# The add of the two halves of V's products, moved from VectorE to GpSimd

## The chip, the core and the metric

The kernel runs on one core of a Trainium2 chip. The metric is the device time of one execution in microseconds, as the median of several runs. The engines of the core that matter here are TensorE (PE in the profile; PEld are its weight loads), VectorE (DVE), ScalarE (ACT), GpSimd (POOL) and SyncE (SP), which only issues transfers. Each works through its own instructions in order, and they wait for each other by semaphores.

## What is computed

An attention block over 16 images of 32 x 32 pixels with 512 channels, all in f32:

```python
xn = silu(group_norm(x, gn_scale, gn_offset))        # 32 groups
q, k, v = split(einsum('bxyc,cd->bxyd', xn, w_qkv), 3)   # 8 heads of 64
sim = einsum('bhdi,bhdj->bhij', q * 64 ** -0.5, k)   # 1024 x 1024 per head
out = einsum('bhij,bhdj->bhid', softmax(sim), v)
return einsum('bxyd,dc->bxyc', out, w_out) + b_out + x
```

## The kernel before

TensorE multiplies f16 operands. To come near f32, each operand is split into a high f16 part and a low one (what the high part left over), and the products of high with high, high with low and low with high are summed in PSUM.

One image is 64 units. A unit is one of eight heads, one half of its 1024 queries and one quarter of its keys (256 keys): `v // 8` is the head, `v // 4 % 2` the half of the queries, `v % 4` the quarter of the keys. Four units are a half: after them the product of the probabilities with V is complete for 512 queries of one head. `step(b, s, ...)` holds 16 units of image `b`; the text counts units of an image from 0 to 63, unit 33 is step 2, `u` = 1. The loop runs over two images at a time and is written out once for every engine, so the order on each is fixed by the code; the tables `TURNS`, `BN_AT`, `Z_AT`, `TANH_AT`, `SILU_FROM` and the like say in which unit side work is done. While image `b` goes through the attention, the group norm, the SiLU and the projections of image `b + 1` are done between.

What each engine does in unit `v`:

- TensorE: the scores (lines 1133 and 1134, into `ST`); the product of the unnormalised scores for a later maximum (line 1045, into `TP`); half of a side job, six passes of a projection (line 1031, into `SD`); and the product of the probabilities of unit `v - 2` with V (line 1163, into `PV`). After units 1, 5, 9, ... it also spreads the shift of a later half over the partitions (line 1052, into `TP`), for which it waits for `ms`.
- ScalarE: the exponentials twice, in f32 (`P`, line 666) and in f16 (`Ph`, line 669); the high part of a side job (`QK` line 623, `V` line 628); `z` and tanh for the SiLU (lines 650, 657). In every unit with `v % 4 == 2` it first copies the finished half from `PV` to `pv_sum` (line 677).
- VectorE: the low part of a side job (lines 769, 774, 781); its half of the low probabilities, `Pl = P - Ph` of unit `v - 1` (line 865); in units with `v % 4 == 3` the function `sums`; the maximum over `TP` (line 828) and, after the fourth maximum of a group, `ms` (line 798). When TensorE has spread the shift, VectorE copies it into `QK2` (line 832).
- GpSimd: the other half of `Pl` of unit `v - 1` (line 553); in units with `v % 4 == 3` the function `normalise`; in units 26 to 47 the SiLU of the next image, three operations in two units (lines 530, 533, 537, 540, each 128x512, from `z` and `th` to the high and low part of `xn`); the bias on the residual (line 545); and once an image the Newton steps and coefficients of the group norm.

V lies in SBUF with its high part, a column of ones, and its low part beside each other: 64 + 1 + 64 columns. The high probabilities are multiplied with all of them, the low ones with the first 65. `PV` thus holds for each of four query blocks a sum for the high part (64 columns), the denominators (one column, `HD`) and a sum for the low part (64 columns from `LO` = 65). The last block has its low part added within PSUM already, so three blocks are left to be added. `pv_sum` (f32, two buffers, by `half % 2`) receives them, `den` the reciprocals of the denominators. `normalise` writes four blocks into `O32`, which TensorE transposes later (line 1105) for the output projection.

The semaphores around it: ScalarE's copy raises `pv_out`; VectorE waits for it in `sums` and raises `den_ready`; GpSimd waits for that in `normalise` and raises `o_normed`; ScalarE waits for `o_normed` before it overwrites the buffer of two halves ago, and TensorE before it transposes. GpSimd's `Pl` raises `lo_pool`, for which TensorE waits before line 1163 and ScalarE before it overwrites `P`.

Of the kernel before, what the change touches and what calls it, by code (L numbers as in the profile page):

```python
# [10 lines left out]
ALU = mybir.AluOpType  # L11
# [4 lines left out]
HEADS, HD = 8, 64  # L16
# [6 lines left out]
LO = HD + 1  # L23
# [23 lines left out]
def rows_of(hh):  # L47

    return slice(hh * HD, hh * HD + HD)
# [151 lines left out]
def wait(eng, sem, count):  # L201

    if not isinstance(count, int) or count > 0:
        eng.wait_ge(sem, count)


def conv_attention(nc, x, gamma, beta, w_qkv, w_out, b_out, out):
# [4 lines left out]
    with ctx:  # L212
        def sb(name, shape, dt):
            return ctx.enter_context(nc.sbuf_tensor(name, shape, dt))
# [4 lines left out]
        def sem(name):  # L219
            return ctx.enter_context(nc.semaphore(name))  # L220
# [48 lines left out]
        pv_sum = sb("pv_sum", [P, 2, 4, LO + HD], F32)  # L269
        den = sb("den", [P, 2, 4], F32)  # L270
# [69 lines left out]
        pv_done = sem("pv_done")  # L340
        pv_out = sem("pv_out")
        den_ready = sem("den_ready")
        o_normed = sem("o_normed")

        def wait_placed(eng, pairs):
# [122 lines left out]
        def _(pool):  # L468
# [86 lines left out]

            def normalise(b, half):

                pool.wait_ge(den_ready, 16 * b + half + 1)
                pair, hh, q = half // 4 % 4, half // 2 % 2, half % 2
                if hh == q == 0:  # L560

                    wait(pool, ot_filled, 4 * b + half // 4 - 1)
                nc.gpsimd.tensor_tensor(O32[:, pair % 2, 4 * q:4 * q + 4, rows_of(hh)],  # L563
                                        pv_sum[:, half % 2, :, 0:HD],
                                        den[:, half % 2, :].unsqueeze(2).to_broadcast([P, 4, HD]), ALU.mult
                                        ).then_inc(o_normed, 1)

            def step(b, s, par, first=False, last=False):
                for u in range(16):
                    v = 16 * s + u  # L570
                    if not (first and v == 0):
                        low_probs(b, v - 1)
                    if v % 4 == 3 and not (first and v == 3):
                        normalise(b, v // 4 - 1)
                    if (s, u) == NEWTON_AT and not last:
                        newton(b + 1)
                        coefficients(b + 1)
                    for i, op in [] if last else silu_ops(s, u):
                        silu(b + 1, 1 - par, i, op)
                    if (s, u) in BIAS_AT:  # L580
                        add_bias(b, BIAS_AT[s, u])
                    if (s, u) in LATE_BIAS_AT and not first:
                        add_bias(b - 1, LATE_BIAS_AT[s, u])
# [8 lines left out]
            with nc.Fori(0, B // 2 - 1, engines=[pool.engine], hint_back_edge=True) as two:  # L592
                b = two * 2
# [10 lines left out]
            for s in range(4):  # L604
                step(B - 1, s, 1, last=True)
            low_probs(B - 1, UNITS - 1)
            normalise(B - 1, 15)
            for t in range(4, 8):
                add_bias(B - 1, t)
# [129 lines left out]
        def _(dve):  # L739
# [128 lines left out]
            def sums(b, half):  # L868


                dve.wait_ge(pv_out, 16 * b + half + 1)
                nc.vector.reciprocal(den[:, half % 2, :], pv_sum[:, half % 2, :, HD])
                nc.vector.tensor_tensor(pv_sum[:, half % 2, 0:3, 0:HD], pv_sum[:, half % 2, 0:3, 0:HD],  # L873
                                        pv_sum[:, half % 2, 0:3, LO:LO + HD], ALU.add).then_inc(den_ready, 1)

            def step(b, s, par, cnt, first=False, last=False):
                turned = []
                for u in range(16):
                    v = 16 * s + u
                    if (s, u) == AGGREGATE_AT and not last:  # L880
                        dve.wait_ge(bn_done, b + 2)
                    for use in (shift_before(s, u, last) if not (first and v == 0) else []):
                        top_use(use, b + 1, cnt)
                    for use in job_before(s, u, first, last):
                        side(use, image_of(use, b, s), cnt)
                    for use, slot in turned:
                        low_output(use[1], image_of(use, b, s), slot)
                    if not (first and v == 0):
                        low_probs(b, v - 1)
                    if v % 4 == 3 and not (first and v == 3):  # L890
                        sums(b, v // 4 - 1)
                    for use in unit_max(s, u, last):
                        top_use(use, b + 1, cnt)
                    cnt.next_slot()
                    turned = [(use, cnt.next_slot()) for use in unit_turn(s, u, first, last)]
                    turned = [(use, slot) for use, slot in turned if use[0] == "ot"]
                    if not last:
                        if (s, u) in BN_AT:
                            for i in BN_AT[s, u]:
                                channel_stats(b + 1, 1 - par, i)  # L900
                        if (s, u) == AGGREGATE_AT:
                            aggregate(b + 1)
                for use in unit_job(s, 15, first, last):
                    side(use, image_of(use, b, s), cnt)
# [97 lines left out]
            with nc.Fori(0, B // 2 - 1, engines=[dve.engine], hint_back_edge=True) as two:  # L1002
                b, now = two * 2, cnt.later(two * 2)
# [11 lines left out]
            for s in range(4):  # L1015
                step(B - 1, s, 1, now, last=True)
            low_probs(B - 1, UNITS - 1)
            sums(B - 1, 15)
            low_output(3, B - 1, now.next_slot())
            for t in range(TB):  # L1020
# [244 lines left out]
```

## Time and profile before

| | us |
|---|---|
| median of 3 runs | 3793.7 |
| lowest and highest | 3792.2 and 3794.3 |
| the profiled execution, its own time | 3788.9 |
| its span in the trace | 3787.1 |
| TensorE busy (matmuls) | 3622.2 (96%) |
| VectorE busy | 3211.4 (85%) |
| ScalarE busy | 2816.3 (74%) |
| GpSimd busy | 2309.0 (61%) |

The granted clock of TensorE is 0.99 of full speed in the mean over the span, and nine tenths or more in every slice of the page but the first. The shares are means over an image whose parts differ: they say which engine is near its limit, not which one is waited for at a given place. For that the waits and the timelines are read. The idle time of an engine is put down to what released it last. A duration on VectorE or GpSimd includes the time in which the instruction had begun but could not yet reach its operands, so the same operation on the same shape may be short in one place and long in another.

### The profile page before, as it was taken

What the parts mean: (1) busy time and instruction counts of PE and PEld (TensorE: products, weight loads), DVE (VectorE), ACT (ScalarE), POOL (GpSimd) and SP (SyncE); (2) the same over time, 40 slices, a digit from 0 to 9 for tenths busy, and PEclk for the clock granted to TensorE, in tenths of its full rate; (3) what the DMA queues carried; (4) which work ended last, traced back from release to release, by engine and by line L of the source; (5) the groups of instructions that cost most, each with busy time, mean ns of one, the idle gap of its engine ahead of it and who ended that gap; (6) DMA issues with size and microseconds to landing.
All of it is one profiled execution on the core that took longest, in us unless ns stands there. A gap on an engine that the chain in (4) does not pass through costs nothing.

```text
span 3787.1 us, 92715 instructions
## 1 busy us (share of the span) xinstructions
PE 3622.2 (96%) x32844; PEld 2103.6 (56%) x32844; DVE 3211.4 (85%) x4027; ACT 2816.3 (74%) x3074; POOL 2309.0 (61%) x2211
## 2 busy tenths in 40 slices
PE   5899999999999999999999999999999999999997
PEld 2555555555555555555555555555555555555553
DVE  6888888888888888888888898888988888888885
ACT  3777777778777787777777777787777877777774
POOL 1383855838467494765838567494764847558444
PEclk7999999999999999999999999999999999999999
DMA  2112113132131222213132121221212222131221
GB/s 92 53 39 77 55 46 85 35 91 57 46 85 40 68 57 71 60 40 87 38 82 62 48 73 40 83 57 53 78 40 68 57 74 57 46 85 35 68 57 34
DMA packets 120776, 228.89 MB, mean 60 GB/s; under 512 B 12672, under 2 KB 29056, under 8 KB 120320
## 3 DMA queue, kind: packets, MB, share of 16 engines
q1 hardware_dynamic: 120320, 222.87, 21.9%
q8 instruction: 279, 4.57, 0.5%
q14 instruction: 177, 1.45, 0.1%
HBM read 71.57 MB, written 33.55 MB: 28 GB/s over the span
## 4 chain that ended last, share of the span: by engine, by line
PE 73%; DVE 14%; issue 7%; ACT 4%; DMA 1%; POOL 0%; DVEq 0%; SPq 0%; ACTq 0%; POOLq 0%
PE SD L1031 26%; PE PV L1163 14%; PE ST L1133 9%; PE ST L1134 9%; PE TP L1045 9%; DVE mx L828 5%; DVE Pl L865 3%; DVE ms L798 2%; PE TP L1052 2%; PE ST L1098 1%; ACT Ph L669 1%; PE ST L1105 1%; DVE st L842 1%; ACT th L657 1%; DVE res L781 1%
## 5 line engine op out<-in xcount | busy, mean ns | idle before, releaser
L553 POOL TENSOR_TENSOR Pl<-P,Ph 128x512 f16<-128x512 f32 x1024 | 1265.1, 1236 | 1171.6 <-ACT Ph L669 1170.5
L666 ACT ACTIVATE P<-ST,cns 128x1024 f32<-128x1024 f32 x1024 | 1141.1, 1114 | 780.0 <-PE ST L1134 767.6
L828 DVE TENSOR_REDUCE mx<-TP 128x1 f32<-128x1024 f32 x1024 | 1244.9, 1216 | 171.9 <-PE TP L1045 168.6
L669 ACT ACTIVATE Ph<-ST,cns 128x1024 f16<-128x1024 f32 x1024 | 1133.7, 1107 | 0.0
L865 DVE TENSOR_TENSOR Pl<-P,Ph 128x512 f16<-128x512 f32 x1024 | 1028.5, 1004 | 9.3 <-ACT Ph L669 6.1
L1163 PE MATMUL PV<-V,Ph 128*128 128x129 f16 (+2 forms) x10240 | 862.5, 210 | 4.4 <-POOL Pl L553 1.6
L1163 PEld LDWEIGHTS PV<-V,Ph 128*128 128x128 f16 x10240 | 771.8, 97 | 125.9 <-ACT pv_sum L677 8.9
L1163 PE MATMUL PV<-V,Pl 128*128 128x65 f16 x8192 | 835.0, 192 | 0.0
L1163 PEld LDWEIGHTS PV<-V,Pl 128*128 128x128 f16 x8192 | 723.1, 98 | 110.3 <-issue 1.1
L1134 PE MATMUL ST<-QK 128*128 128x512 f16 x2048 | 777.5, 380 | 2.6 <-issue 2.6
L1133 PE MATMUL ST<-QK 128*128 128x512 f16 x2048 | 777.6, 380 | 0.3 <-ACT Ph L669 0.2
L1031 PE MATMUL SD<-X,wq 128*128 128x512 f16 x3048 | 745.2, 381 | 21.5 <-POOL X L521 15.6
L1045 PE MATMUL TP<-QK 128*128 128x512 f16 x2048 | 610.4, 380 | 14.7 <-DVE mx L828 11.7
L1031 PEld LDWEIGHTS SD<-X,wq 128*128 128x128 f16 x3048 | 291.0, 98 | 403.0 <-DVE QK L769 47.7
L1031 PE MATMUL SD<-wo,OT 128*128 128x512 f16 x1536 | 374.7, 381 | 10.9 <-DVE res L781 8.4
L1031 PE MATMUL SD<-wq,X 128*128 128x512 f16 x1488 | 361.4, 379 | 1.3 <-DVE wq L929 1.3
L1133 PEld LDWEIGHTS ST<-QK 128*128 128x128 f16 x2048 | 202.6, 99 | 184.0 <-issue 1.9
L1134 PEld LDWEIGHTS ST<-QK 128*128 128x128 f16 x2048 | 200.2, 98 | 181.6 <-issue 1.3
L769 DVE SCALAR_TENSOR_TENSOR QK<-SD,sc,QK 128x512 f16<-128x512 f32 x254 | 190.2, 749 | 118.6 <-ACT QK L623 102.4
L832 DVE CAST QK<-TP 64x512 f16<-64x512 f32 x256 | 176.1, 688 | 133.8 <-PE TP L1052 132.1
L563 POOL TENSOR_TENSOR O<-pv_sum,den 128x256 f32<-128x256 f32 x256 | 157.6, 616 | 199.1 <-DVE pv_sum L873 199.1
L1031 PEld LDWEIGHTS SD<-wo,OT 128*128 128x128 f16 x1536 | 149.0, 98 | 199.7 <-DVE res L781 19.1
(110 smaller groups left out, 3222.3 us busy)
## 6 DMA issues: line engine op xcount, KB each, us to landing
QK<-QK SPq DMA_DIRECT2D x384, 256.0 KB, 4.9
res<-in_x SPq DMA_DIRECT2D x128, 256.0 KB, 2.8
out<-res SPq DMA_DIRECT2D x128, 256.0 KB, 2.0
x_in<-in_x SPq DMA_DIRECT2D x61, 512.0 KB, 3.9
V<-V SPq DMA_DIRECT2D x16, 1040.0 KB, 6.4
V<-in_L_conv_w_qkv SPq DMA_DIRECT2D x4, 768.0 KB, 11.0
P<-in_L_conv_w_out SPq DMA_DIRECT2D x1, 1024.0 KB, 14.7
z<-in_x SPq DMA_DIRECT2D x1, 512.0 KB, 6.1
```

Source lines behind the costliest of these rows:

```text
L553: nc.gpsimd.tensor_tensor(Pl[:, v % 4, HALF:], P32[:, v % 2, HALF:], Ph[:, v % 4, HALF:], ALU.subtract).then_inc(lo_pool, 1)
L666: nc.scalar.activation(P32[:, v % 2, :], ST[:, slot, :], ACT.Exp, scale=cns[:, 0:1])
L669: nc.scalar.activation(Ph[:, v % 4, :], ST[:, slot, :], ACT.Exp, scale=cns[:, 0:1]).then_inc(exp_done, 1)
L769: nc.vector.scalar_tensor_tensor(out=QK[:, lo, cols], in0=bank, scalar=sc[:, col:col + 1], in1=QK[:, hi, cols], op0=ALU.mult, op1=ALU.subt ...
L828: nc.vector.reduce_max(mx[:, hh, qb:qb + 1], TP[:], AX.X).then_inc(top_drained, 1)
L832: nc.vector.tensor_copy(QK2[r, head_slot(pair, hh), 0, bass.ts(half, HALF)], TP[r, 0:HALF]).then_inc(top_drained, 1)
L865: nc.vector.tensor_tensor(Pl[:, v % 4, 0:HALF], P32[:, v % 2, 0:HALF], Ph[:, v % 4, 0:HALF], ALU.subtract).then_inc(lo_dve, 1)
L1031: ins = nc.tensor.matmul(bank, stationary(i, c), moving(j, c), start=(c == 0 and i + j == 0), stop=(c == CC - 1 and i == 1))
L1045: ins = nc.tensor.matmul(TP[:, bass.ts(kh, HALF)], QK1[:, slot, 0, bass.ts(qb, P)], QK1[:, slot, 1, bass.ts(kh, HALF)], start=True, stop=True)
L1133: nc.tensor.matmul(dst, QK1[:, at, 1, kb], QK1[:, at, 0, bass.ts(q, HALF)], start=True, stop=False)
L1134: ins = nc.tensor.matmul(dst, QK2[:, at, 1, kb], QK2[:, at, 0, bass.ts(q, HALF)], start=False, stop=True)
L1163: ins = nc.tensor.matmul(PV[:, cols], stationary, moving, start=kb == qb == n == 0, stop=kb == TB - 1, skip_group_check=True)
```

## The change

In `sums` VectorE keeps the reciprocals and raises `den_ready` behind them. The add of the three low parts to the high parts, in place in `pv_sum`, goes to the head of `normalise` on GpSimd, behind a wait of its own for `pv_out`. A new semaphore, `pv_added`, lets GpSimd's normalisation wait for GpSimd's own add; behind it stands the wait for `den_ready` as before. Shapes and types are the same. The order of everything else on the five engines stays.

```diff
--- before.py
+++ after.py
@@ -340,6 +340,7 @@
         pv_done = sem("pv_done")
         pv_out = sem("pv_out")
         den_ready = sem("den_ready")
+        pv_added = sem("pv_added")
         o_normed = sem("o_normed")
 
         def wait_placed(eng, pairs):
@@ -555,6 +556,10 @@
 
             def normalise(b, half):
 
+                pool.wait_ge(pv_out, 16 * b + half + 1)
+                nc.gpsimd.tensor_tensor(pv_sum[:, half % 2, 0:3, 0:HD], pv_sum[:, half % 2, 0:3, 0:HD],
+                                        pv_sum[:, half % 2, 0:3, LO:LO + HD], ALU.add).then_inc(pv_added, 1)
+                pool.wait_ge(pv_added, 16 * b + half + 1)
                 pool.wait_ge(den_ready, 16 * b + half + 1)
                 pair, hh, q = half // 4 % 4, half // 2 % 2, half % 2
                 if hh == q == 0:
@@ -869,9 +874,7 @@
 
 
                 dve.wait_ge(pv_out, 16 * b + half + 1)
-                nc.vector.reciprocal(den[:, half % 2, :], pv_sum[:, half % 2, :, HD])
-                nc.vector.tensor_tensor(pv_sum[:, half % 2, 0:3, 0:HD], pv_sum[:, half % 2, 0:3, 0:HD],
-                                        pv_sum[:, half % 2, 0:3, LO:LO + HD], ALU.add).then_inc(den_ready, 1)
+                nc.vector.reciprocal(den[:, half % 2, :], pv_sum[:, half % 2, :, HD]).then_inc(den_ready, 1)
 
             def step(b, s, par, cnt, first=False, last=False):
                 turned = []
```

On VectorE, in units 35 and 36 (`Pl` of unit 34, then `sums`, the maximum, the low part of a side job). Before:

```order
L865 TENSOR_TENSOR Pl<-P,Ph 128x512 [waits pv_done]
L871 ISA
L872 RECIPROCAL den<-pv_sum 128x4 [waits pv_out]
L873 TENSOR_TENSOR pv_sum<-pv_sum 128x3x64
L803 REGISTER_ALU
L828 TENSOR_REDUCE mx<-TP 128x1 [waits top_filled]
L759 REGISTER_ALU
L762 REGISTER_ALU [waits side_filled]
L769 SCALAR_TENSOR_TENSOR QK<-SD,sc,QK 128x512 [waits placed1,placed0,side_hi]
```

And with the change, whose lines are numbered 4 or 5 higher there:

```order
L870 TENSOR_TENSOR Pl<-P,Ph 128x512 [waits pv_done]
L876 ISA
L877 RECIPROCAL den<-pv_sum 128x4 [waits pv_out]
L808 REGISTER_ALU
L833 TENSOR_REDUCE mx<-TP 128x1 [waits top_filled]
L764 REGISTER_ALU
L767 REGISTER_ALU [waits side_filled]
L774 SCALAR_TENSOR_TENSOR QK<-SD,sc,QK 128x512 [waits placed1,placed0,side_hi]
```

The add is gone and the maximum stands directly behind the reciprocals; nothing else moved.

On GpSimd, in the same units (`Pl` of unit 34, `normalise`, an operation of the SiLU, `Pl` of unit 35). Before:

```order
L553 TENSOR_TENSOR Pl<-P,Ph 128x512 [waits pv_done,exp_done]
L558 REGISTER_ALU
L563 TENSOR_TENSOR O<-pv_sum,den 128x4x64 [waits den_ready]
L536 REGISTER_ALU
L537 TENSOR_TENSOR z<-z,th 128x512 [waits silu_step]
L550 REGISTER_ALU
L553 TENSOR_TENSOR Pl<-P,Ph 128x512 [waits pv_done,exp_done]
```

And with the change:

```order
L554 TENSOR_TENSOR Pl<-P,Ph 128x512 [waits pv_done,exp_done]
L559 REGISTER_ALU
L560 TENSOR_TENSOR pv_sum<-pv_sum 128x3x64 [waits pv_out]
L568 TENSOR_TENSOR O<-pv_sum,den 128x4x64 [waits den_ready,pv_added]
L537 REGISTER_ALU
L538 TENSOR_TENSOR z<-z,th 128x512 [waits silu_step]
L551 REGISTER_ALU
L554 TENSOR_TENSOR Pl<-P,Ph 128x512 [waits pv_done,exp_done]
```

The add stands between `Pl` and the normalisation, and the SiLU's operation and the next `Pl` stand behind both.

## Rows read from the trace of the kernel before

**Rows 1.** the page: busy time, share of the span, instructions of each engine.

```profile
PE 3622.2 (96%) x32844; PEld 2103.6 (56%) x32844; DVE 3211.4 (85%) x4027; ACT 2816.3 (74%) x3074; POOL 2309.0 (61%) x2211
```

**Rows 2.** busy time by stretch: image 6, units 0-23, 24-47 and 48-63.

```profile
core 0: us, PE busy (x) PEld busy (x) DVE busy (x) ACT busy (x) POOL busy (x), PEclk, DMA share, GB/s
1472.85:1560.19 87.34, 86.36 (x790) 50.93 (x787) 75.14 (x106) 63.08 (x68) 39.87 (x53) 1.00 0.26 74
1560.19:1646.48 86.29, 83.14 (x765) 48.22 (x762) 75.92 (x87) 71.15 (x80) 80.66 (x64) 1.00 0.25 63
1646.48:1701.92 55.44, 55.04 (x513) 31.78 (x510) 46.12 (x59) 41.29 (x46) 25.96 (x25) 1.00 0.17 39
```

**Rows 3.** waits by engine and line: us in total, times, longest.

```profile
POOL Pl L553 <- ACT Ph L669: 1170.5, 650, 37.6
...
PE TP L1052 <- DVE ms L798: 72.1, 97, 2.5
...
PE ST L1105 <- POOL O L563: 1.8, 1, 1.8
```

**Rows 4.** VectorE by line, duration in ns, least/median/most.

```profile
L865 DVE TENSOR_TENSOR Pl<-P,Ph x1024: 667/834/1747, 104.2 to 3744.3; 128x512 f16<-128x512 f32 x171
...
L873 DVE TENSOR_TENSOR pv_sum<-pv_sum x256: 321/325/1351, 128.2 to 3747.7; 128x192 f32<-128x192 f32 x128
...
L798 DVE TENSOR_SCALAR ms<-mx,cns x256: 228/230/1106, 93.8 to 3729.2; 128x4 f16<-128x4 f32 x128
```

**Rows 5.** groups by line: busy us, mean ns, idle before.

```profile
L563 POOL TENSOR_TENSOR O<-pv_sum,den 128x256 f32<-128x256 f32 x256 | 157.6, 616 | 199.1 <-DVE pv_sum L873 199.1
L873 DVE TENSOR_TENSOR pv_sum<-pv_sum 128x192 f32<-128x192 f32 x256 | 152.1, 594 | 0.0
```

**Rows 6.** timeline, VectorE, units 35 to 37: start us, us, line.

```profile
1599.12 1.22 DVE L873 TENSOR_TENSOR pv_sum<-pv_sum 128x192 f32<-128x192 f32 x1
...
1602.59 0.75 DVE L769 SCALAR_TENSOR_TENSOR QK<-SD,sc,QK 128x512 f16<-128x512 f32 x1 [1.11 <-ACT QK L623]
1603.26 0.68 DVE L865 TENSOR_TENSOR Pl<-P,Ph 128x512 f16<-128x512 f32 x1
...
1604.99 1.73 DVE L865 TENSOR_TENSOR Pl<-P,Ph 128x512 f16<-128x512 f32 x1
...
1607.89 1.10 DVE L798 TENSOR_SCALAR ms<-mx,cns 128x4 f16<-128x4 f32 x1
```

**Rows 7.** timeline, GpSimd, the same stretch.

```profile
1600.42 0.62 POOL L563 TENSOR_TENSOR O<-pv_sum,den 128x256 f32<-128x256 f32 x1 [0.30 <-DVE pv_sum L873]
...
1602.23 1.16 POOL L553 TENSOR_TENSOR Pl<-P,Ph 128x512 f16<-128x512 f32 x1
...
1604.92 1.26 POOL L530 TENSOR_TENSOR th<-z,th 128x512 f32<-128x512 f32 x1
...
1607.70 1.26 POOL L533 TENSOR_TENSOR X<-z,th 128x512 f16<-128x512 f32 x1
```

**Rows 8.** timeline, GpSimd and VectorE, units 31 to 33.

```profile
1585.83 0.61 POOL L563 TENSOR_TENSOR O<-pv_sum,den 128x256 f32<-128x256 f32 x1
...
1589.19 1.26 POOL L533 TENSOR_TENSOR X<-z,th 128x512 f16<-128x512 f32 x1
1590.54 1.27 POOL L537 TENSOR_TENSOR z<-z,th 128x512 f32<-128x512 f32 x1
...
1593.33 1.16 POOL L540 TENSOR_TENSOR X<-z,X 128x512 f16<-128x512 f32 x1
...
1591.56 0.79 DVE L865 TENSOR_TENSOR Pl<-P,Ph 128x512 f16<-128x512 f32 x1
...
1593.52 0.99 DVE L798 TENSOR_SCALAR ms<-mx,cns 128x4 f16<-128x4 f32 x1
```

**Rows 9.** timeline, GpSimd and VectorE, behind unit 39.

```profile
1615.34 0.62 POOL L563 TENSOR_TENSOR O<-pv_sum,den 128x256 f32<-128x256 f32 x1 [1.36 <-DVE pv_sum L873]
...
1617.08 0.75 DVE L769 SCALAR_TENSOR_TENSOR QK<-SD,sc,QK 128x512 f16<-128x512 f32 x1 [1.08 <-ACT QK L623]
```

## The prediction

> **What bounds the kernel now.** I read the busy shares first, then the three stretches of one image, then the waits, and last the timelines of VectorE and GpSimd where TensorE waits. TensorE is busy in 96% of the span [rows 1], so a change on other engines can only reach what is left. Image 6, cut into three [rows 2], shows where that is. In its first 87.3 us TensorE lacks 1.0 us of being busy and in the last 55.4 us it lacks 0.4, while in the middle 86.3 us (units 24 to 47, where GpSimd does the SiLU of the next image) it lacks 3.2 us. GpSimd is busy for 80.7 of those 86.3 us, against 39.9 and 26.0 in the other two. The longest wait of TensorE is for `ms` at line 798, 72.1 us in 97 waits [rows 3]. It is the shift: the maxima of four query blocks must be reduced and scaled before TensorE may go on to the next scores. So VectorE bounds TensorE at four places of an image (the shifts of units 33, 37, 41, 45), and hardly elsewhere.
>
> **What bounds VectorE there.** Two things, and the removed add is neither. First, its two-input operations and GpSimd's exclude each other. VectorE's `Pl` takes 0.67 us at best and 1.75 at worst, the add at line 873 0.32 and 1.35, the little `ms` 0.23 and 1.11 [rows 4]. In the timelines each long one of VectorE ends just after a GpSimd operation does: `Pl` from 1604.99 lasts 1.73 us because line 530 runs on GpSimd from 1604.92 to 1606.18, and `ms` from 1607.89 lasts 1.10 because line 533 runs until 1608.96 [rows 6, 7]. Second, VectorE waits for work: behind the add and the maximum of unit 35 it stands 1.11 us until ScalarE has written `QK` [rows 6].
>
> **What the change removes.** 256 adds on VectorE, 0.594 us each in the mean, 152 us in all [rows 5]. The median is 0.325 us [rows 4]; the others stand behind a GpSimd operation. To bring TensorE anything, this time would have to lie in an unbroken run up to a shift. At unit 35 it doesn't: the add ends at 1600.34, the maximum behind it at about 1601.5, and then VectorE waits until 1602.59 for ScalarE [rows 6]. Without the add that wait is 1.1 us longer, and `QK`, `Pl` and the shift come when they came. Behind unit 39 it waits 1.08 us for `QK` [rows 9], behind unit 43 for ScalarE's half of `V`, and behind unit 31 for TensorE's product. So I take the gain at 0. Its bound from the other side: all of the wait for `ms` gone, 72 us [rows 3].
>
> **What it adds to GpSimd.** 256 adds of 128x192. No such row stands in the trace. The normalisation, 128x256 with the same two inputs in f32, takes 0.616 us [rows 5]. That is the upper bound, and by the number of elements it would be 0.616 x 192/256 = 0.46, the lower one. I take 0.48. Between the add and the normalisation GpSimd waits for its own semaphore. The dependent pair of lines 533 and 537 shows what that costs: from 1590.45, the end of 533, to 1590.54, 0.09 us [rows 8], so 0.56 us in all, 143 us over the run. The Trainium skill, GPSIMD Engine Reference, section "Performance versus the Vector engine", gives GpSimd 1.96 times VectorE's time for a two-input f32 add, and calls VectorE the engine for elementwise work. By it the add would take 0.325 x 1.96 = 0.64 us, which is above the row of the larger normalisation, so the rows decide; with 0.64 each of the three delays below would be 0.16 us larger, 7 us in all.
>
> **Where GpSimd has room.** Outside the SiLU stretch it waits for each pair of exponentials (1170.5 us in 650 waits before line 553 [rows 3]) and the 0.56 us vanish in that. The reader of its result is some way off: TensorE turns `O32` thirteen, five, one and one units after its last normalisation, and waited for it once in the whole run [rows 3]. ScalarE, which also waits for `o_normed` before it overwrites `pv_sum`, does so two halves (eight units) later. Behind the new wait for `pv_out` stand the SiLU pieces and the next `Pl` on GpSimd's queue, but ScalarE has written `pv_sum` a unit earlier, so that wait is over when it is reached.
>
> **Where it has none.** In the SiLU stretch its operations stand end to end, and what it is given moves all behind it, up to the next place where it would have waited.
> - Units 31 to 33. At unit 31 the normalisation starts at 1585.83 without a wait [rows 8], so all of the 0.56 us counts, less about 0.1 for a `Pl` that VectorE's add no longer holds up. Line 537 ends not at 1591.81 but about 1592.3. VectorE asks for `Pl` at 1591.56, is held until 537 ends, and this is the unbroken run to the shift: `Pl`, maximum, `ms`, held again by line 540 behind it until 1594.49 [rows 8]. All moves by 0.5 us, and TensorE waits 0.5 us longer. Laid out in the same way for image 7, the rows give 0.5 again.
> - Units 35 to 37. Here GpSimd waited 0.30 us for VectorE's add before its normalisation at 1600.42 [rows 7]. The new add can start at about 1600.1, when `Pl` ends, and the normalisation follows at 1600.65, so the delay is 0.23 us. GpSimd's `Pl` then ends at 1603.6 instead of 1603.39. VectorE asks at 1603.26 [rows 6]; it was let in at 1603.39 [rows 7] and is now let in 0.24 us later. `Pl`, maximum, `Pl` (held by 530), maximum, `ms` (held by 533) is again unbroken: +0.24 us.
> - Units 39 to 41 and 43 to 45. At unit 39 GpSimd waited 1.36 us for VectorE's add [rows 9], and now it starts 0.4 us or more ahead of where it was. By the order of requests this may put its `Pl` in front of VectorE's (the 0.68 us one becomes 1.35, +0.7) or change nothing. For units 43 to 45 I get between -0.2 and +0.1. The two together are between -0.2 and +0.7 an image; most of what I can lay out gives nearly nothing in one image and more in the next, and I take +0.1.
>
> **Sum.** 0.5 + 0.24 + 0.1 = 0.84 us for each of the 15 images that have this stretch, 12.6 us; the first and last image's edges add nothing that can be told. The profiled execution took 3788.9 us (span 3787.1), which gives 3801.5. The median of the three runs, 3793.7, lies 4.9 us above it, and the same 12.6 put on it are 3806.
>
> **Rivals.**
> 1. The terms cancel. The order in which the two engines ask decides each hold-up, and a shift of 0.2 us can turn either way; images 6 and 7 already differ in it. Time 3794, within 7.6. For it: the stretch lengthens by 0.5 us at unit 33, which gives GpSimd time to catch up. Against: the first two terms come out alike in both images.
> 2. GpSimd falls out of step to VectorE's advantage. In the shifts of units 33 and 37 `ms` takes 0.99 and 1.10 us [rows 6, 8] where 0.23 is possible [rows 4], close to the worst there is, and the other two look the same. If one of the four escapes, some 0.85 x 15 = 13 us are won: 3781. Against: as long as GpSimd has no gap, `Pl` on VectorE hands over to a GpSimd operation of 1.16 or 1.27 us, and `ms` asks 1.2 us later, just when the next one has begun. The pattern holds itself.
> 3. VectorE's relief counts in full: 0.594 us on each of 97 waits, 58 us at most, minus the places above: about 3745. It needs the add to be in the unbroken run; the 1.11 us wait for `QK` speaks against it.
> 4. GpSimd becomes the bound of the SiLU stretch. 80.7 us and five or six times 0.56 are 83.8 of 86.3 us, and it is held up by VectorE besides. From the point where it has no gap between units 25 and 47, `Pl` and the SiLU pieces come late for TensorE and ScalarE, and the stretch grows by what is added, 2 us an image: 3794 + 30 = 3824. Against: GpSimd's wait of 1.36 us at unit 39 is such a gap.
>
> **How the numbers follow.** Forecast (delays of 0.5 to 1.4 us an image, 3801 to 3815) 0.48; rival 1 0.25; rival 2 0.17; rival 3 0.04; rival 4 0.06. A measurement of this kernel can tell about 0.2%, 7.6 us, from no change. Faster by more: 0.17 + 0.04 = 0.21. Within: 0.25. Slower by more: 0.48 + 0.06 = 0.54. The range leaves out rival 3 and the outer part of rivals 2 and 4: 3779 to 3822.
>
> **What would show it.** In the changed kernel's profile: GpSimd's add at 0.46 to 0.5 us where nothing holds it; VectorE's busy time lower by 150 us or somewhat less, with its idle time before `QK` (line 769 of before) higher; GpSimd's wait before the normalisation nearly gone; the wait of TensorE for `ms` up from 72 to about 85 us, in the shifts of units 33 and 37 of every image; stretches outside the SiLU unchanged in length. The forecast is wrong if the middle stretch of image 6 doesn't grow, if `ms` is found at 0.23 us in one of the four shifts, or if GpSimd's new add takes over 0.62 us.

## The result, and the profile after

The changed kernel takes 3807.4 us, median of 7 runs (3806.6 to 3809.4), against 3793.7 of the kernel before (7 runs, 3791.0 to 3796.7): 13.7 us longer, ratio 1.0037 with a 95% interval of 1.0026 to 1.0049. The forecast was 3806. The profiled execution took 3807.5 us (span 3805.8), 18.7 us more than that of before; the profiled run of before lies 4.9 us below its median, so the medians are the measure, and the trace is read by stretches.

Line numbers of the changed kernel are 1 higher for most of GpSimd's lines (5 for the normalisation), 5 for VectorE's and ScalarE's, 3 for TensorE's. First the busy times of its page (compare [rows 1]):

```profile
PE 3627.0 (95%) x32844; PEld 2105.7 (55%) x32844; DVE 3139.5 (82%) x3771; ACT 2818.8 (74%) x3074; POOL 2501.4 (66%) x2467
```

VectorE lost 72 us, from 3211 to 3140, not the 152 that the adds had taken, and GpSimd gained 192, not 256 x 0.52 = 133. Most of the rest is the holding-up, since each engine's time contains its waits for the other: VectorE's 1024 `Pl` took 1028.5 us in all before and take 1077.5 now. A part is that operations overlap in the records: a `Pl` begins some 0.1 us before the recorded end of the one in front. Now image 6 in the same three stretches (units 0 to 23, 24 to 47, 48 to 63; columns as in [rows 2]):

```profile
core 0: us, PE busy (x) PEld busy (x) DVE busy (x) ACT busy (x) POOL busy (x), PEclk, DMA share, GB/s
1479.85:1566.81 86.96, 86.32 (x790) 50.94 (x787) 73.78 (x100) 63.13 (x67) 43.63 (x58) 1.00 0.25 74
1566.81:1654.85 88.04, 83.51 (x765) 48.29 (x762) 74.60 (x81) 71.20 (x81) 84.96 (x71) 1.00 0.24 61
1654.85:1709.94 55.09, 55.04 (x513) 31.79 (x510) 45.39 (x55) 41.32 (x46) 29.69 (x29) 1.00 0.17 40
```

The middle stretch is 1.75 us longer (88.04 against 86.29), and the two others are 0.38 and 0.35 us shorter, since in images of even number a small wait of TensorE behind units 20 and 50 went. The image is 230.09 us long against 229.07. Image 7, an odd one, grew from 228.93 to 229.98; in it nothing but the middle stretch moved, from 86.89 to 87.92. (Images are counted from 0. The length of one runs from its first exponential to that of the next.) From the second to the fourteenth image each is 0.97 to 1.09 us longer, 13.4 us together.

The waits (us in total, times, longest; compare [rows 3]):

```profile
PE TP L1055 <- DVE ms L803: 86.0, 98, 3.0
...
DVE QK L774 <- ACT QK L628: 133.0, 139, 7.5
```

TensorE's wait for `ms` rose from 72.1 to 86.0 us. VectorE's wait for ScalarE's `QK` stood at 102.4 us in 132 waits before: a part of the time that VectorE was relieved of is found there. The new add (ns: least/median/most):

```profile
L560 POOL TENSOR_TENSOR pv_sum<-pv_sum x256: 516/974/1000, 127.8 to 3766.2; 128x192 f32<-128x192 f32 x128
```

It takes 0.516 us where nothing holds it. More than half of the 256 take 0.97, because VectorE's `Pl` has the access first. Outside the SiLU stretch that is idle time of GpSimd. Inside it the adds of units 27, 31 and 35 take 0.52 us, and those of units 39, 43 and 47 take 0.97.

Where it hurts is seen in the timelines. GpSimd and VectorE in units 31 to 33 of image 6 (start us, us; this is what [rows 8] show for before; all lies some 7.4 us later):

```profile
1592.60 0.52 POOL L560 TENSOR_TENSOR pv_sum<-pv_sum 128x192 f32<-128x192 f32 x1
1593.20 0.62 POOL L568 TENSOR_TENSOR O<-pv_sum,den 128x256 f32<-128x256 f32 x1
...
1597.92 1.27 POOL L538 TENSOR_TENSOR z<-z,th 128x512 f32<-128x512 f32 x1
...
1600.72 1.15 POOL L541 TENSOR_TENSOR X<-z,X 128x512 f16<-128x512 f32 x1
...
1598.40 1.34 DVE L870 TENSOR_TENSOR Pl<-P,Ph 128x512 f16<-128x512 f32 x1
...
1600.91 0.98 DVE L803 TENSOR_SCALAR ms<-mx,cns 128x4 f16<-128x4 f32 x1
```

The SiLU's operation behind which VectorE stands (line 538, was 537) ends at 1599.19. VectorE asked at 1598.40 and was held 0.55 us longer than before (`Pl` 1.34 us, was 0.79), and `ms` is held by line 541 as it was (0.98, was 0.99). Units 35 to 37 (compare [rows 6, 7]):

```profile
1607.48 0.52 POOL L560 TENSOR_TENSOR pv_sum<-pv_sum 128x192 f32<-128x192 f32 x1
1608.08 0.62 POOL L568 TENSOR_TENSOR O<-pv_sum,den 128x256 f32<-128x256 f32 x1
...
1609.89 1.16 POOL L554 TENSOR_TENSOR Pl<-P,Ph 128x512 f16<-128x512 f32 x1
...
1609.98 0.75 DVE L774 SCALAR_TENSOR_TENSOR QK<-SD,sc,QK 128x512 f16<-128x512 f32 x1 [1.78 <-ACT QK L628]
1610.65 0.95 DVE L870 TENSOR_TENSOR Pl<-P,Ph 128x512 f16<-128x512 f32 x1
...
1612.65 1.73 DVE L870 TENSOR_TENSOR Pl<-P,Ph 128x512 f16<-128x512 f32 x1
...
1615.55 1.10 DVE L803 TENSOR_SCALAR ms<-mx,cns 128x4 f16<-128x4 f32 x1
```

Add and normalisation follow `Pl` without a gap. GpSimd's next `Pl` ends at 1611.05, 0.40 us after VectorE's asking; it was 0.13. VectorE's `Pl` takes 0.95 instead of 0.68, the next one 1.73 and `ms` 1.10 as before. VectorE waits 1.78 us for `QK`, where it waited 1.11.

And what TensorE sees of it: its shift of units 33, 37, 41 and 45 of image 6, with the idle time in brackets. Before:

```profile
1594.57 0.40 PE L1052 MATMUL TP<-ident,ms 128*128 128x128 f16 x4 [0.84 <-DVE ms L798]
...
1609.05 0.40 PE L1052 MATMUL TP<-ident,ms 128*128 128x128 f16 x4 [0.81 <-DVE ms L798]
...
1624.12 0.40 PE L1052 MATMUL TP<-ident,ms 128*128 128x128 f16 x4 [0.61 <-DVE ms L798]
...
1638.60 0.40 PE L1052 MATMUL TP<-ident,ms 128*128 128x128 f16 x4 [0.88 <-DVE ms L798]
```

After:

```profile
1601.95 0.40 PE L1055 MATMUL TP<-ident,ms 128*128 128x128 f16 x4 [1.39 <-DVE ms L803]
...
1616.71 0.40 PE L1055 MATMUL TP<-ident,ms 128*128 128x128 f16 x4 [1.08 <-DVE ms L803]
...
1632.60 0.40 PE L1055 MATMUL TP<-ident,ms 128*128 128x128 f16 x4 [1.44 <-DVE ms L803]
...
1646.96 0.40 PE L1055 MATMUL TP<-ident,ms 128*128 128x128 f16 x4 [0.27 <-DVE ms L803]
```

The waits in brackets are not all of the delay, since the recorded end of the matmuls in front overlaps it. The distance from one shift to the next shows the whole. At units 25 and 29 of image 6, before:

```profile
1565.71 0.39 PE L1052 MATMUL TP<-ident,ms 128*128 128x128 f16 x4
...
1579.13 0.39 PE L1052 MATMUL TP<-ident,ms 128*128 128x128 f16 x4
```

After, where the weight load of the second waits for `ms`:

```profile
1572.34 0.39 PE L1055 MATMUL TP<-ident,ms 128*128 128x128 f16 x4
...
1585.96 0.40 PE L1055 MATMUL TP<-ident,ms 128*128 128x128 f16 x4
...
1585.96 0.23 PEld L1055 LDWEIGHTS TP<-ident,ms 128*128 128x128 f16 x4 [0.16 <-DVE ms L803]
```

That is 13.42 us before and 13.62 after. In the mean over the seven odd images from 1 to 13, the distances up to the shifts of units 29, 33, 37, 41 and 45 grew by 0.20, 0.49, 0.25, 0.06 and 0.05 us, 1.05 together, and the eleven others by nothing that can be told. In the six even ones between them the same five grew by 0.20, 0.56, 0.26 and 0.83 us and shrank by 0.12, and 0.73 us went behind units 20 and 50: 1.00 together.

### The profile page after: what moved, and what is told of

The parts are those of the page before. It is cut to its first block and busy times, and to the rows that moved or that the text cites. A ratio compares the mean times of both kernels' runs of the same rounds, so it can differ in the third digit from the quotient of the medians.

```text
span 3805.8 us, 92951 instructions
## 1 busy us (share of the span) xinstructions
PE 3627.0 (95%) x32844; PEld 2105.7 (55%) x32844; DVE 3139.5 (82%) x3771; ACT 2818.8 (74%) x3074; POOL 2501.4 (66%) x2467
## 5 line engine op out<-in xcount | busy, mean ns | idle before, releaser
L870 DVE TENSOR_TENSOR Pl<-P,Ph 128x512 f16<-128x512 f32 x1024 | 1077.5, 1052 | 16.7 <-ACT Ph L674 12.6
L1034 PEld LDWEIGHTS SD<-wq,X 128*128 128x128 f16 x1488 | 142.1, 98 | 181.4 <-DVE V L779 14.3
```

The source lines that it names most:

```text
L870: nc.vector.tensor_tensor(Pl[:, v % 4, 0:HALF], P32[:, v % 2, 0:HALF], Ph[:, v % 4, 0:HALF], ALU.subtract).then_inc(lo_dve, 1)
L1034: ins = nc.tensor.matmul(bank, stationary(i, c), moving(j, c), start=(c == 0 and i + j == 0), stop=(c == CC - 1 and i == 1))
```

## Experiments

Theory 1 is the prediction's: the cost is that GpSimd comes late in the SiLU stretch and so holds VectorE's operations in front of a shift for longer, and VectorE's relief is worth nothing. Theory 2 says that the relief is worth something, and what is seen is the difference of two larger things. Theory 3 puts the cost on the longer path to `o_normed`. The kernel before ran beside each group on the same chip, and medians are compared with that.

**No add at all.** The low half's part is left out of the output on both engines.

```diff
-                nc.vector.reciprocal(den[:, half % 2, :], pv_sum[:, half % 2, :, HD])
-                nc.vector.tensor_tensor(pv_sum[:, half % 2, 0:3, 0:HD], pv_sum[:, half % 2, 0:3, 0:HD],
-                                        pv_sum[:, half % 2, 0:3, LO:LO + HD], ALU.add).then_inc(den_ready, 1)
+                nc.vector.reciprocal(den[:, half % 2, :], pv_sum[:, half % 2, :, HD]).then_inc(den_ready, 1)
```

> The add of the low half's products is left out on both engines: VectorE does the reciprocals alone and GpSimd normalises the sum of the high half only. Theory 1 (the change costs because GpSimd is late in the SiLU stretch, and VectorE's relief is worth nothing, since VectorE waits for ScalarE or TensorE between the removed add and the shift): within 4 us of before, 3790 to 3798. Theory 2 (VectorE's relief is worth something, and GpSimd's lateness costs more than the 13.7 us that are seen): 10 us or more faster than before, 3784 or less, and the waits for ms fall.

Measured: 3786.7 us against 3791.9, ratio 0.9985 (0.9976 to 0.9995). So the relief is worth 5 us, of 152 us of VectorE's time: more than the 0 of theory 1, half of what theory 2 asked for. The lengths of the images say where. Odd ones are as long as before (228.92 us in the mean against 228.94), even ones 0.43 us shorter (228.82 against 229.25). From image 1 to 13 that makes 2.7 us; the rest stands in the parts that differ between any two profiles (the last section has them). The timelines say why so little. Taking the add away gave VectorE another phase against GpSimd. Units 28 and 29 of image 6, GpSimd and then VectorE:

```profile
1575.14 1.26 POOL L530 TENSOR_TENSOR th<-z,th 128x512 f32<-128x512 f32 x1
...
1577.93 1.27 POOL L533 TENSOR_TENSOR X<-z,th 128x512 f16<-128x512 f32 x1
...
1575.21 1.74 DVE L865 TENSOR_TENSOR Pl<-P,Ph 128x512 f16<-128x512 f32 x1
...
1578.12 1.10 DVE L798 TENSOR_SCALAR ms<-mx,cns 128x4 f16<-128x4 f32 x1
```

`Pl` asks 0.07 us after line 530 has begun and is held for all of it (1.74 us), and so is `ms` behind it (1.10). In the kernel before the same two took 0.85 and 0.41 us there, and TensorE did not wait. Its shifts in this kernel, from unit 29 to unit 45:

```profile
1579.28 0.40 PE L1050 MATMUL TP<-ident,ms 128*128 128x128 f16 x4 [0.65 <-DVE ms L798]
...
1594.06 0.40 PE L1050 MATMUL TP<-ident,ms 128*128 128x128 f16 x4 [0.18 <-DVE ms L798]
...
1608.21 0.40 PE L1050 MATMUL TP<-ident,ms 128*128 128x128 f16 x4 [0.26 <-DVE ms L798]
...
1624.14 0.40 PE L1050 MATMUL TP<-ident,ms 128*128 128x128 f16 x4 [1.47 <-DVE ms L798]
...
1638.20 0.40 PE L1050 MATMUL TP<-ident,ms 128*128 128x128 f16 x4 [0.27 <-DVE ms L798]
```

0.65 us of waiting where there was none, and 1.47 at unit 41 instead of 0.61, against 0.66, 0.55 and 0.61 us won at units 33, 37 and 45 (0.84, 0.81 and 0.88 before). The waits behind units 20 and 50 (0.33 and 0.38) went as well, as they did with the change. In image 7 unit 33 won nothing (1.06 us, 0.98 before).

**An extra add on GpSimd**, with VectorE's add kept.

```diff
+                pool.wait_ge(pv_out, 16 * b + half + 1)
+                nc.gpsimd.tensor_tensor(spare[:], pv_sum[:, half % 2, 0:3, LO:LO + HD],
+                                        pv_sum[:, half % 2, 0:3, LO:LO + HD], ALU.add).then_inc(pv_added, 1)
+                pool.wait_ge(pv_added, 16 * b + half + 1)
                 pool.wait_ge(den_ready, 16 * b + half + 1)
```

> VectorE as before, with its add; GpSimd does an add of the same shape on top, behind its own wait for pv_out, into a spare tile (its result is not used). Theory 1: all of the cost is GpSimd's, so 12 to 18 us slower than before, 3806 to 3812; the stalls at the shifts of units 33 and 37 grow by 0.4 to 0.7 and 0.2 to 0.3 us. Theory 2: more than the change cost, by what the relief gave it, 3817 or more. Theory 3 (what costs is the path from pv_out to o_normed, which the extra add lengthens as the change did): the same time too, but with the wait of TensorE for O at its transposes up.

Measured: 3814.7 us against 3791.9, 22.8 us longer, ratio 1.0059 (1.0042 to 1.0076). Theory 1's 12 to 18 us are too few, and theory 2's 3817 was 23.3 above before, which is as good as met: GpSimd's part alone costs more than the whole change. The stalls at the shifts of units 33 and 37 of image 6 grew by 0.65 and 0.36 us (from 0.84 and 0.81 to 1.49 and 1.17). With the 5 us of the first experiment the two parts make 22.8 - 5.2 = 17.6 us, against 13.7 measured; the intervals, 6.5 and 3.6 us each way, allow that. By images the two experiments say more. Odd images are 1.10 us longer with the extra add (230.04 against 228.94) and 1.06 longer with the change (230.00), and without the add they are what they were: there all of the cost is GpSimd's and the relief is worth nothing, as theory 1 has it. Only in even images is there a difference of two things, 1.70 us for the extra add and 0.43 for the relief, where the change cost 1.00. Theory 3 falls. TensorE's waits in this kernel:

```profile
PE TP L1058 <- DVE ms L804: 92.0, 97, 3.0
...
PE ST L1111 <- POOL O L569: 2.6, 2, 2.2
```

The wait for `O` is 2.6 us in 2 waits, as good as nothing, while that for `ms` is 92.0.

**The add moved only outside the SiLU stretch, and only inside.** One list decides per half on which engine the add is done; the waits count the moved ones.

```diff
+        moved = [5, 6, 7, 8, 9, 10]
...
+                if half % 16 in moved:
+                    pool.wait_ge(pv_out, 16 * b + half + 1)
+                    nc.gpsimd.tensor_tensor(pv_sum[:, half % 2, 0:3, 0:HD], pv_sum[:, half % 2, 0:3, 0:HD],
+                                            pv_sum[:, half % 2, 0:3, LO:LO + HD], ALU.add).then_inc(pv_added, 1)
+                    pool.wait_ge(pv_added, len(moved) * b + sum(h <= half for h in moved))
```

The other kernel has the other ten halves in the list. Outside:

> The add is moved to GpSimd in the ten halves of an image outside the SiLU stretch (those that end before units 3 to 23 and 51 to 63), and stays on VectorE in the six halves normalised in units 27 to 47. Theory 1: as before, 3790 to 3798. A cost spread evenly over all 256 adds (semaphores, the longer chain): 10/16 of 13.7 us, 3802.

Inside:

> The converse: moved only in the six halves normalised in units 27 to 47. Theory 1: the whole cost, 3804 to 3811, with the stalls of the changed kernel at all four shifts. Spread evenly: 6/16 of 13.7 us, 3799.

Measured: outside 3795.5 us, ratio 1.0008 (0.9998 to 1.0017), no difference that can be told; inside 3806.1, ratio 1.0037 (1.0022 to 1.0051), the whole cost. Image 6 of the kernel with the ten adds outside, in the three stretches:

```profile
1474.31:1561.27 86.96, 86.32 (x790) 50.95 (x787) 73.80 (x100) 63.13 (x67) 43.65 (x58) 1.00 0.26 74
1561.27:1648.21 86.94, 83.38 (x765) 48.17 (x762) 76.52 (x87) 71.20 (x81) 80.80 (x65) 1.00 0.24 62
1648.21:1703.31 55.10, 55.05 (x513) 31.75 (x510) 45.40 (x55) 41.33 (x46) 29.70 (x29) 1.00 0.16 40
```

It is 229.00 us long, and before it was 229.07. The stretches moved against each other (-0.4, +0.65, -0.3 us, the other pattern of an even image, on which more below), the sum didn't, although GpSimd is 3.8 us busier in the first stretch and 3.7 in the last. Of the 3.6 us by which the median lies above that of before, the images from 1 to 13 show nothing: odd ones are within 0.1 us of before, even ones 0.1 us shorter. With the six adds inside, image 6 is 230.04 us, as in the changed kernel. This settles where the cost arises.

**Two halves, and one half.** The list is `[5, 6]` (normalised in units 27 and 31), then `[7]` (unit 35).

> The add is moved to GpSimd in two halves of an image alone, those normalised in units 27 and 31. By the prediction's laying out, and with what the changed kernel showed: the stalls at the shifts of units 29 and 33 grow by 0.2 and 0.5 us as in the changed kernel, and the later two or three stay as before; an image 0.6 to 0.7 us longer, the run 9 to 11 us. If instead each place hangs on all adds before it, the shift of unit 37 grows too (by 0.24).

> Moved in the half normalised in unit 35 alone. Theory 1: nothing at the shifts of units 29 and 33, +0.24 us at that of unit 37, the run 3 to 4 us longer, which only the lengths of the images in the trace can tell. If the shift of unit 37 needs GpSimd to be late already: 0.

Measured: 3801.9 us against 3792.7 for the two, ratio 1.0025 (1.0014 to 1.0035); 3796.6 for the one, 1.0012 (1.0001 to 1.0022). The lengths of the images tell more than the medians. Odd images grew by 0.63 to 0.70 us with the two and by 0.20 to 0.29 with the one; even ones by 0.54 to 0.63 and by about 0.5. In the odd images the stalls grew by 0.2 and 0.5 us at units 29 and 33 with the first list, by 0.25 at unit 37 with the second, and nowhere else. So the terms add up place by place: 0.66 + 0.25 = 0.91 of the 1.05 us by which an odd image grew with the whole change. The even images are less plain. In them the shift of unit 41 came 0.77 us later in both kernels, and other waits fell by 0.5 to 0.9 us. With the first list that is the whole change from one of the two patterns of stalls to the other; with the second it is a part of it, since the wait behind unit 50 (0.38 us) stayed. From shift to shift, the whole change of pattern makes an even image 0.13 us shorter (0.78 more, and 0.17, 0.37 and 0.37 less), so that 0.74 - 0.13 = 0.61 us is what the first list cost one.

**Without `ms`.** The maxima are written as bf16 and TensorE spreads them as they are; offset and factor are applied in the copy from PSUM into `QK2`, which has to be made anyway. The identity matrix of that product is bf16 too, and VectorE's operation `ms` and TensorE's wait for it are gone.

```diff
-        mx = sb("mx", [P, 2, TB], F32)
-        ms = sb("ms", [P, 2, TB], F16)
+        mx = sb("mx", [P, 2, TB], BF16)
...
-                    nc.vector.tensor_copy(QK2[r, head_slot(pair, hh), 0, bass.ts(half, HALF)], TP[r, 0:HALF]
-                                          ).then_inc(top_drained, 1)
+                    nc.vector.tensor_scalar(QK2[r, head_slot(pair, hh), 0, bass.ts(half, HALF)], TP[r, 0:HALF],
+                                            cns[r, 3:4], -1.0 / (HD * ROWC), ALU.subtract, ALU.mult
+                                            ).then_inc(top_drained, 1)
...
-                    pe.wait_ge(shift_ready, cnt.shifts + 1)
...
-                        ins = nc.tensor.matmul(TP[:, bass.ts(i, P)], ms[:, hh, qb:qb + 1].to_broadcast([P, P]),
+                        ins = nc.tensor.matmul(TP[:, bass.ts(i, P)], mx[:, hh, qb:qb + 1].to_broadcast([P, P]),
```

> Kernel before without the operation ms on VectorE: the maxima are written as bf16 and TensorE spreads them as they are; offset and factor of the shift are applied in the copy out of TP, which VectorE does anyway and which reads PSUM. Theory 1 (the stalls at the shifts end with an ms that GpSimd holds up): each stall shrinks by the time of its ms, 0.8 to 1.1 us, so 3 to 4 us of the middle stretch of an image and 0.7 at units 1 and 9 go: 50 to 70 us, 3722 to 3742. If it was the chain in front of ms that was late, whatever stands at its end, and GpSimd's hold only lay beside it: 0.23 us in five places, 17 us, 3775.

Measured: 3725.5 us against 3792.7, ratio 0.9821 (0.9805 to 0.9838), 67 us faster, and faster than both kernels of this case. An operation on 128x4 elements, which takes 0.23 us where nothing holds it, held up the kernel by 1.8%. How much of that is its being held by GpSimd, and how much its own time and one more hand-over in the chain, the run doesn't part; theory 1's 50 to 70 us are met, the other's 17 are not. Image 6 in the three stretches:

```profile
1450.46:1536.54 86.08, 85.92 (x790) 50.68 (x787) 73.43 (x100) 62.97 (x68) 39.47 (x53) 1.00 0.25 75
1536.54:1620.89 84.35, 83.35 (x765) 47.87 (x762) 74.67 (x81) 71.22 (x81) 81.71 (x64) 1.00 0.25 64
1620.89:1675.80 54.91, 54.89 (x513) 31.62 (x510) 45.48 (x55) 41.19 (x45) 26.80 (x25) 1.00 0.17 40
```

The middle stretch is 84.35 us, before it was 86.29, and TensorE lacks 1.0 us of being busy in it instead of 3.2. So it is 1.9 us shorter, where 3 to 4 were expected, and the two others are 1.8 us shorter together (1.26 and 0.53), where 0.7 was expected: the sum came true, its parts did not. The shifts of units 33 to 45:

```profile
1569.91 0.39 PE L1049 MATMUL TP<-ident,mx 128*128 128x128 bf16 x4
...
1584.26 0.40 PE L1049 MATMUL TP<-ident,mx 128*128 128x128 bf16 x4
...
1598.63 0.40 PE L1049 MATMUL TP<-ident,mx 128*128 128x128 bf16 x4
...
1613.00 0.40 PE L1049 MATMUL TP<-ident,mx 128*128 128x128 bf16 x4 [0.15 <-DVE mx L825]
```

Of the four waits (0.84, 0.81, 0.61, 0.88) one of 0.15 is left, and two others, of 0.26 and 0.42 us behind units 35 and 43, have come, in which TensorE waits for the maximum. GpSimd and VectorE exclude each other as before in `Pl`; it is the last link in front of TensorE that is gone.

The same with the add on GpSimd:

> The same with the add on GpSimd. Theory 1: GpSimd's lateness still moves VectorE's Pl in front of the shifts of units 33 and 37, but with the stall in front of TensorE gone, most of it finds room: 0 to 7 us slower than the same kernel with the add on VectorE. If the cost of the move doesn't hang on the stalls: 13 to 15 us slower than it.

Measured: 3736.5 us, 11.0 more than the same kernel with the add on VectorE, ratio to before 0.985 (0.9834 to 0.9867). I had expected 0 to 7. The images from 1 to 13 are longer by 0.33 to 0.77 us each, 8.1 us together, where the change cost them 13.4. So without `ms` the move still costs six to eight tenths of what it did (8.1 of 13.4, and 11.0 of 13.7 in the medians), and the account of place by place does not carry over. From shift to shift an odd image takes 0.63 us more up to unit 33, 0.92 less up to unit 37 and 0.63 more up to unit 41, and 0.36 us of its 0.76 arise in units 17 to 21, outside the SiLU stretch. The waits of TensorE that are left are mostly for the maximum and for `QK`, so the chain in front of `ms` is again the last to arrive; which of its operations GpSimd holds up there was not followed.

## Why the prediction was right

- **The bound.** Confirmed. TensorE's busy time hardly moved (3622 to 3627 us), and the stretches outside the SiLU grew by nothing. That holds for odd images; in even ones the two other stretches shrank by 0.38 and 0.35 us with the change of pattern. The two kernels that moved the add outside or inside of the stretch alone showed it directly: +3.6 us (not told from 0) and +14.2.
- **VectorE's relief, taken at 0.** Right for odd images, 0.43 us too little for even ones; 5 us in the medians of the kernel without any add. The reason given (VectorE then waits for ScalarE) holds at unit 35, where the wait for `QK` went from 1.11 to 1.78 us. It was incomplete: the earlier VectorE meets GpSimd at other moments, which in image 6 wins at the shifts of units 33, 37 and 45 and loses at those of units 29 and 41. That this comes to nearly nothing was not worked out, and is in part luck. The sign that went with it failed: VectorE's busy time was to fall by 150 us or somewhat less and fell by 72, since the time in which its `Pl` is held rose.
- **The new operation, 0.48 us.** It takes 0.516 at least, within the bounds 0.46 and 0.616 for one that nothing holds. That it would mostly be held (0.97 us in the median) was not foreseen. The text named more than 0.62 us as a sign of a wrong forecast; it was a poor sign, since it is GpSimd's idle time where it is long, outside the SiLU stretch. The dependent normalisation follows 0.08 us behind the add's end (1593.12 to 1593.20), where 0.09 was taken.
- **Units 31 to 33, +0.5 us.** Measured +0.55 in VectorE's `Pl` and +0.55 in the idle time before TensorE's shift (0.84 to 1.39). In image 7 it is +0.47 (0.98 to 1.45).
- **Units 35 to 37, +0.24 us.** Measured +0.27 (0.81 to 1.08), and 0.24 in image 7 (0.89 to 1.13).
- **Units 39 to 45, between -0.2 and +0.7, taken +0.1.** In image 7 it is +0.1. In image 6 the waits went from 0.61 to 1.44 and from 0.88 to 0.27, and one of 0.32 us came in front of the product for the maximum of unit 45. From shift to shift that is +0.7 us, and with the 0.73 us that went behind units 20 and 50 the rest of an even image comes to about 0. The reason given for a large term, GpSimd coming early to unit 39, is not what did it: the kernels that left unit 39 alone show the same +0.8 us at unit 41. GpSimd's normalisation there came 0.26 us earlier against the shift of unit 37, not 0.4 or more, because the add took 0.97 us. So the +0.1 is right for odd images, and for even ones the 0 is luck.
- **Unit 29, left out.** There TensorE did not wait before. `ms` now takes 0.69 instead of 0.41 us, and from the shift of unit 25 to that of unit 29 it is 13.62 us instead of 13.42. This is the term that the sum lacks, 0.2 us an image, 3 us in all.
- **The sum.** 0.84 us an image were forecast and 1.03 measured, 12.6 and 15.4 us over 15 images. The medians differ by 13.7. That they lie so close to the 12.6 is in part luck, since a term of 3 us was missing.
- **Rivals.** The terms did not cancel, although the shuffling that rival 1 and 2 spoke of is real and moves single shifts by up to 0.8 us. GpSimd did not become the bound: it is busy for 85.0 of 88.0 us, but TensorE waited for its `Pl` only 2.3 us in the whole run.

## What to carry over

When two engines exclude each other, what an operation costs is not its own time but where the other engine's next request falls; busy shares say nothing on that, and the two timelines beside each other at the place that waits say most of it. Moving work off an engine with idle time behind it wins next to nothing, and giving it to one whose operations stand end to end is paid at the next place where that one holds up somebody. Look at the last small operation in front of a wait: if it only scales a few numbers, fold it into one that reads PSUM and has to run anyway.

## What the runs showed of the hardware

- When VectorE and GpSimd both wait for access, VectorE is let in as soon as GpSimd's running operation ends, even if GpSimd's next one has begun: behind `Pl` of unit 35, line 541 begins on GpSimd at 1611.01 and takes 1.60 us instead of 1.16, while VectorE's `Pl` runs. In the profile of before, each of the 543 `Pl` of VectorE that were held for 0.1 us or more began while a GpSimd operation ran, and all but one end when they would if let in at the end of that operation. Then GpSimd has the access for its whole operation, and VectorE's next request falls into it. That would make the pattern keep itself, and mostly it does; but without the add `ms` of unit 33 took 0.23 us in the even images, so it can be broken.
- The reciprocal of 128x4 (0.165 us, 0.179 at most), the maximum over PSUM (1.21) and the operations with one input in PSUM (line 769: 0.75 at most) were never held. `ms`, one input of 128x4 in SBUF, was: it took up to 1.11 us before and up to 1.33 in the changed kernel. The Trainium skill, SBUF — State Buffer, section "SBUF: two separate sides", says that an operation with two inputs in SBUF, or one in a mode that uses both ports, shares its access with GpSimd, and that the loser waits for the whole instruction; the rows of `Pl` and the add agree. For `ms`, which has one such input, no row tells in which mode it runs; that it waits, with four columns, is seen.
- In the kernel before, images alternated between two patterns of stalls (229.1 to 229.4 us and 228.9 to 229.0), and several edits, whatever they were meant for, changed that of the even images: the wait at unit 41 up by 0.8 us, others down by as much. A difference at one shift of one image says little by itself.
- Some parts differ from one profiled execution to the next by more than the 1 us or so that the edits cost an image. In the eight kernels with `ms`, what stands ahead of image 0 takes 101.0 to 103.0 us, image 0 itself 225.0 to 229.2, image 14 230.9 to 235.7, and what comes behind it 246.8 to 254.0. Between the profiles of the two kernels of this case, images 0 and 14 grew by 1.8 and 2.8 us, and by that the profiled times differ by 18.7 us where the medians differ by 13.7. What causes it was not tried.
